# X16 and XT16 read back from memory by one transfer of 512 KB each instead of two of 256 KB

## The reference, cut to what matters

```
def step(state, inp):
    q_t, k_t, v_t, g_t, b_t = inp
    state = state * jnp.exp(g_t)[..., None, None]
    kv_mem = jnp.einsum('bhkv,bhk->bhv', state, k_t)
    delta = (v_t - kv_mem) * b_t[..., None]
    state = state + jnp.einsum('bhk,bhv->bhkv', k_t, delta)
    o = jnp.einsum('bhkv,bhk->bhv', state, q_t)
    return (state, o)
```

## Time and profile before

| | us |
|---|---|
| runs of the kernel before | 3132.66, 3140.78, 3145.97 |
| their median | 3140.78 |
| the profiled execution | 3115.73 |
| span of its instructions on the core | 3113.7 |
| busy in it: PE, DVE, POOL, ACT | 2886.9, 2733.2, 2050.0, 1871.7 |

### The profile page before, as it was taken

How to read it: one execution, slowest core, us unless ns; L and a number is a source line. 1 busy time by engine, 2 the same in 40 slices (tenths; PEclk the granted TensorE clock), 3 DMA queues, 4 the chain that set the end, 5 groups by cost and what they waited for, 6 DMA issues and landing times.

```text
span 3113.7 us, 56444 instructions
## 1 busy us (share of the span) xinstructions
PE 2886.9 (93%) x18444; PEld 2386.7 (77%) x18444; DVE 2733.2 (88%) x9037; ACT 1871.7 (60%) x4431; POOL 2050.0 (66%) x2397
## 2 busy tenths in 40 slices
PE   7851899999999999999999999999999999999997
PEld 4431688888888888888888888888888888888886
DVE  4997799999998989989998999899998999988895
ACT  4320566666666666666666666666665666666663
POOL 0003677777776777767777777777777777777764
PEclk9985899999999999999999999999999999999998
DMA  2001555555555555555554555555555555555552
GB/s 63 1 1 45 133 138 134 143 144 138 144 135 135 143 139 138 133 137 143 145 138 128 143 144 144 134 137 143 145 138 133 137 144 145 138 144 131 141 143 81
DMA packets 524419, 394.22 MB, mean 127 GB/s; under 512 B 245984, under 2 KB 449760, under 8 KB 524128
## 3 DMA queue, kind: packets, MB, share of 16 engines
q0 software_dynamic: 65536, 201.39, 24.6%
q1 hardware_dynamic: 458592, 189.23, 23.6%
HBM read 345.41 MB, written 45.09 MB: 125 GB/s over the span
## 4 chain that ended last, share of the span: by engine, by line
PE 46%; DVE 34%; DMA 14%; issue 3%; POOL 1%; ACT 1%; SPq 1%; POOLq 1%; DVEq 0%; ACTq 0%
PE ps L550 12%; DMA X<-whole 7%; PE ps L573 7%; PE ps L516 7%; PE ps L566 7%; DVE mix L1237 6%; DMA whole<-xr 6%; PE ps L533 4%; PE ps L540 3%; DVE xr L1253 3%; DVE MT L1313 3%; DVE outer L1249 2%; DVE qkv L1195 2%; DVE prod L1259 2%; DVE prod L1273 2%
## 5 line engine op out<-in xcount | busy, mean ns | idle before, releaser
L965 POOL DMA_INDIRECT rows<-table,idx_all x1024 | 1106.1, 1080 | 572.5 <-DVEq L1343 294.6
L550 PEld LDWEIGHTS ps<-X,AT 128*128 128x128 f32 x3072 | 365.2, 195 | 84.2 <-DMA X<-whole 83.3
L550 PE MATMUL ps<-X,AT 128*128 128x128 f32 x3072 | 388.2, 280 | 32.3 <-DMA X<-whole 31.2
L573 PE MATMUL ps<-XT,E 128*128 128x128 f32 x3072 | 400.7, 277 | 0.0
L1237 DVE SCALAR_TENSOR_TENSOR mix<-rows,zc,mix 128x256 f32<-128x256 f32 x896 | 376.3, 484 | 2.5 <-ACT zc L828 2.5
L573 PEld LDWEIGHTS ps<-XT,E 128*128 128x128 f32 x3072 | 369.2, 192 | 0.0
L1195 DVE SCALAR_TENSOR_TENSOR qkv<-raw,cwkq,qkv 128x510 f32<-128x510 f32 (+2 forms) x384 | 288.3, 751 | 63.3 <-ACT qkv L807 54.2
L806 ACT ACTIVATE raw<-ps 128x512 f32<-128x512 f32 x256 | 152.8, 597 | 310.9 <-PE ps L516 310.9
L957 POOL TENSOR_SCALAR gm<-cst,gn 128x128 f32<-128x128 f32 x512 | 316.2, 630 | 6.7
L949 POOL TENSOR_SCALAR xg<-xg,rms 128x128 f32<-128x128 f32 x520 | 311.8, 611 | 7.0
L566 PEld LDWEIGHTS ps<-E,XT 128*128 128x128 f32 x2048 | 259.8, 192 | 60.6 <-issue 59.8
(11 more groups left out here) (167 smaller groups left out, 6306.8 us busy)
## 6 DMA issues: line engine op xcount, KB each, us to landing
Wvz<-wvz SPq DMA_DIRECT2D x64, 512.0 KB, 3.3
whole<-AT SPq DMA_DIRECT2D x128, 256.0 KB, 4.0
X<-whole SPq DMA_DIRECT2D x128, 256.0 KB, 4.1
XT<-whole SPq DMA_DIRECT2D x128, 256.0 KB, 5.4
wo<-woh SPq DMA_DIRECT2D x65, 256.0 KB, 3.6
Wkq<-wkq SPq DMA_DIRECT2D x64, 256.0 KB, 2.6
rows<-table,idx_all POOLq DMA_INDIRECT x1024
bk<-whole SPq DMA_DIRECT2D x64, 64.0 KB
```

The costliest lines, as they stand in the source:

```text
L550: done = mm(ps[:, g, (a % 4) * P:(a % 4 + 1) * P], AT_b[:, a, :], src[:, a, :], start=True, stop=True)
L573: done = mm(ps[:, 4 + g, (a % 4) * P:(a % 4 + 1) * P], E[:, a, :], src[:, a, :], start=True, stop=True)
L965: pool.indirect_dma_start(rows[:, m, :], None, table[:, :], bass.IndirectOffsetOnAxis(ap=idx_all[:, f // 4, c:c + 1], axis=0)).then_inc(ga ...
```

## The change

Each tile is read by one transfer over all eight tasks, in place of two over four tasks. The semaphore counts follow: a transfer adds 16 when it has landed, so inv_in and invt_in go up by 16 in a pass and not by 32.

```
-                   blocks_out=32, blocks_in=16, inv_out=16, inv_in=32, invt_out=16, invt_in=32)
+                   blocks_out=32, blocks_in=16, inv_out=16, inv_in=16, invt_out=16, invt_in=16)
...
                 sp.wait_ge(sm["inv_out"], at("inv_out", 16))
-                for g in range(2):
-                    sp.dma_start(X16[:, 4 * g:4 * g + 4, :], matrices(1, g)).then_inc(sm["inv_in"], 16)
+                sp.dma_start(X16[:, :, :], matrices(1)).then_inc(sm["inv_in"], 16)
                 sp.wait_ge(sm["invt_out"], at("invt_out", 16))
-                for g in range(2):
-                    sp.dma_start(XT16[:, 4 * g:4 * g + 4, :], matrices(2, g)).then_inc(sm["invt_in"], 16)
-                sp.wait_ge(sm["inv_in"], at("inv_in", 32))
-                sp.wait_ge(sm["invt_in"], at("invt_in", 32))
+                sp.dma_start(XT16[:, :, :], matrices(2)).then_inc(sm["invt_in"], 16)
+                sp.wait_ge(sm["inv_in"], at("inv_in", 16))
+                sp.wait_ge(sm["invt_in"], at("invt_in", 16))
```

## The result

The changed kernel takes 3108.77 us in the median of 7 runs (3104.49 to 3117.09), the kernel before 3132.66 us in the median of 7 (3122.11 to 3145.97). The ratio is 0.9924, with a 95% interval of 0.9903 to 0.9945: 0.8% faster, where no change was forecast and 3118 us was the lower end of the range.

What follows compares the result with a forecast made beforehand. The prediction took X16's landing, on the path through PE, to bound the kernel. Its terms, 0 + 1.6 + 0 = 1.6 us less, turned 3140.8 us into 3139 us, with a range of 3118 to 3165 us.

Steps and rivals of the forecast that it cites:

- What bounds the kernel: X16's landing is on the path; 0.1 us earlier is worth at most 3.9 us, later up to 6.3 us.
- Part 1: SP's issues: about 0.96 us in place of 2.0, hidden behind SP's wait for XT16; 0 us on the path.
- Part 2: X16's landing: second half follows the first at the engines' pace; one transfer lands 0.04 us earlier, 1.6 us gained.
- the cost of splitting: In X16's landing: 0.07 us left between the halves' landing step and their bytes' time; half was taken as gain.
- The written-out tile: Zeroed tile of the same shape: data flow within about 1.1 us of issue, so an eight-task list starts in time.
- My margin of 0.1 us: Doubt on X16's landing from judging a read by a write: 3.9 us less or 6.3 us more.
- Part 3: XT16's landing: issued about 0.5 us earlier but behind the same X16 bytes, so it lands as before; 0 us.
- The second: Rival: one list per tile cures 11 late X16 landings, 14 us and up to 15 of clock; 3112 to 3127 us; 0.06.
- The fourth: Rival: one X16 transfer lands 0.17 us later, as two streams no longer overlap; 11 us, 3152 us; chance 0.05.
- The third: Rival: late X16 landings spread ahead of L550; 22 more late passes cost 40 us, 3180 us; chance 0.12.

Runs made afterwards that it cites:

- e3: The kernel before with X16 alone read by one transfer, XT16 still in two halves: 3101.6 us, ratio 0.9873 to the kernel before.
- e4: The kernel before with XT16 alone read by one transfer, X16 still in two halves: 3147.0 us, ratio 1.0022 to the kernel before.
- e1: The kernel before, unchanged, run again as a control: 3137.6 us, ratio 0.9987.
- e8: The changed kernel with the last gather of each pass left out: 3118.5 us, ratio 0.9978 to the kernel before.
- e7: The kernel before, in halves, with the last gather of each pass left out: 3098.8 us, ratio 0.9932 to the kernel before.
- e11: The changed kernel with the last two gathers of a pass issued in POOL's next pass: 3107.7 us, ratio 0.9777 to the kernel before.
- e10: The kernel before, in halves, with the last two gathers of a pass issued in POOL's next pass: 3093.5 us, ratio 0.9731.
- e15: The kernel before, in halves, with POOL holding its last two gathers until SP has made both X16 issues: 3061.4 us, ratio 0.9767.
- e13: The changed kernel, run again on the chip of e14 to e16: 3119.3 us, ratio 0.9956 to the kernel before.
- e16: The kernel before, with SP making X16's second issue only after POOL has issued its last gather of the pass: 3203.5 us, ratio 1.0224.
- e5: The kernel before with both tiles still in two transfers, but cut into even and odd partitions over all eight tasks: 3192.9 us, ratio 1.0235.
- e14: The kernel before, in halves, with the last two gathers issued in the next pass, as e10 on another chip: 3068.7 us, ratio 0.9792.
- e12: The kernel before with two more matmuls on PE, result overwritten, ahead of its wait for X16: 3163.6 us, ratio 0.997.

## Why the prediction was wrong

**What bounds the kernel: right.** X16's landing is on the path, and e3 against e4 shows that nothing else of this change is. But 3.9 us for 0.1 us was read off the waits alone. The same 31.2 us had to be split by pass: 16.5 us of it lay in 10 passes and 3.0 us in the last one, and what moves those moves also the clock.

**Part 1, SP's issues: right.** 0.38 us each, and the saved time lies behind SP's wait ahead of Wvz, which the trace splits in two. Before it is 305.0 us and 5.9 us at L339, after

```profile
SPq L340 <- DMA XT<-whole: 310.4, 63, 5.9
...
SPq L339 <- DVE qkv L1193: 64.6, 62, 1.3
```

so 64 us more in all, where 60 were forecast. The measured gap to XT16's issue is 0.64 us in the pass shown, not 0.46.

**Part 2, X16's landing: this step failed, in two ways.** I asked whether the second half was late because of its issue 0.42 us behind the first or because the engines were full, saw full slices, and concluded that "both halves lie in the queue when the stream begins" and that "the second follows the first at the engines' pace". That holds in the ordinary pass that I had read. The issue gap was weighed as a time, of which the full stream leaves nothing. It is a place in an order: POOL issues a gather at nearly the same moment, and in most passes in which it is the earlier, its 192 KB come before or among the second half. By the measure of 5.85 us that makes 10 to 17 of 62 passes late, at over 1 us each. So late landings, which the sum put at nothing and a rival at 0.06, were the term that decided: e1 against e3 has 22.3 us of waits and 8.4 us of clock in it. The rows for it were there, POOL's issues in order of time beside SP's: the gather 0.27 us behind SP's first issue in the late pass of rows 13, and 0.45 us behind it in the ordinary one of rows 5. I compared the traffic of the two and not the issues.

The term itself, 1.6 us of gain in the ordinary pass, has the wrong sign. With one list X16 lands later than with two: 5.05 against 4.80 us in e8 and e7, 0.6% of the time, and 0.46% in e11 and e10. What I took for the cost of splitting (0.07 us; the mean of the seven slices is 340 and not 344 GB/s, which makes it 0.06) is less than what goes the other way. The written-out tile did not show it, since nothing there compares one list with two. My margin of 0.1 us for "a write where ours is a read" was too narrow. Whether the list itself costs this or XT16's earlier issue stays open. The figures of 2.0 us and 436 GB/s are given in the Trainium skill ("DMA: Bandwidth & Descriptors", in "Anatomy of one DMA") for transfers issued from GpSimd, and X16's are issued from SP.

**Part 3, XT16: right.** e4 measures 1.0022 for it alone, with 1 across its interval.

**The rivals.** The second, the cure of late landings, is what happened. It was priced at 3112 to 3127 us, and 3108.8 us lies just below that; I gave it 0.06 because I could "not tell from the trace what makes them". Its price was about right for the profile that I had (14 us of waits and up to 15 of clock). It was small beside other runs: the control's waits are 50.3 us where that profile's were 31.2, so a profile that was 25 us faster than the median of its runs should have been read as one with fewer late passes than usual, not scaled. The fourth, X16 0.17 us later, also happened, at 0.2 to 0.25 us, and hides part of the gain. The cause given for it, the overlap of two streams, is not shown. The third, late passes that spread, did not come by the measure of 5.85 us, and the argument against it (same bytes, same order) missed that the order among queues changes.

**What would have shown it.** X16's ordinary landing (5.1, neither 4.5 to 4.7 nor 4.2) told that part 2 was wrong. The count of late ones, taken as I had written it, misleads: 20 of the 50 landings in the chain after are over 5.3 us, and 20 or more were to speak for the third rival. I had named the 5.3 us from pieces that count from the second issue, and after the change they count from the first. Over all passes, both counted from the first issue, landings over 5.3 us went from 14 to 20, and PE's starts over 5.85 us from 10 to 1: the middling ones became more and the very late ones went.

## What to carry to other kernels

When two engines issue transfers at nearly the same moment, compare the order of their issues pass by pass, not the mean time to landing: splitting a transfer on which the critical engine waits opens a place for another engine's transfer to get in between. One transfer closes that place at some cost of its own; holding the other engine's transfer back with a semaphore until the critical ones are issued (e15) keeps the halves and closes it too, and was worth 2.3% here, against 0.4% for the one transfer on the same chip (e13). A wait that is short in the mean but long in a few passes must be priced with the clock that can fall behind it, and a profile that is faster than the runs around it shows less of that tail than they have.

## What the runs showed of the hardware that was not expected

- With X16 in two lists, a gather issued less than 0.425 us behind the first half made 24 of 26 passes late (over 5.3 us), one issued later 2 of 36 (e1; 11 of 20 and 3 of 42 in the profile of before). With one list, a gather issued ahead of XT16's list moved its data behind X16 in 60 of 62 passes (after).
- A list issued behind a gather needs longer until its stream runs: about 2 us with a gather ahead, 2.7 us in e16, against under 1 us with none.
- One list of 512 KB in rows of 512 B landed 0.25 us later than two of 256 KB issued 0.42 us apart (e8 and e7), with the next list of the queue issued 0.37 us earlier as well.
- The clock fell to 1.2 GHz for 3.4 us behind idle times of TensorE as short as 0.90 us (e5) and 0.97 us (e14), and not behind each longer one (in e1 behind 5 of the 17 waits for X16 over 1.3 us, and behind one of 1.22); with two short matmuls ahead of the wait, behind none of 17 (e12).
- The same kernel before took 3124.8, 3134.5, 3142.2 and 3173.4 us in the median on four chips.
